# A mixer's small jobs in another order on five queues: where each stands among sixteen steps

## The reference, cut to what matters

```python
h = _layernorm(x, axis=-1) * (1 + ca) + sa
x = x + ga * _L1_attn_ref(h, ...)      # linear attention: elu(q)+1, elu(k)+1
h = _layernorm(x, axis=-1) * (1 + cb) + sb
x = x + gb * _L1_ffn_ref(h, ...)
# _L1_ffn_ref:
src = x + _gqa(x, ...)                 # softmax attention, 16 heads, 4 key heads
src = _rmsnorm(src, norm1_w)
src = src + _moe(src, ...)             # top 2 of 8 experts, capacity 2560, order of tokens counts
return _rmsnorm(src, norm2_w)
```

## Time and profile before

| what | value |
|---|---|
| time, median of 3 runs | 3388.16 us |
| lowest and highest | 3386.55, 3393.27 us |
| the profiled execution's own time | 3381.69 us |
| its span in the profile | 3380.0 us |
| mean granted clock of TensorE | 0.972 |
| busy: TensorE, DVE, ACT, POOL | 93%, 62%, 49%, 33% |

### The profile page before, as it was taken

How to read it: one execution, slowest core, us unless ns; L and a number is a source line. 1 busy time by engine, 2 the same in 40 slices (tenths; PEclk the granted TensorE clock), 3 DMA queues, 4 the chain that set the end, 5 groups by cost and what they waited for, 6 DMA issues and landing times. The chain is left out here.

```text
span 3380.0 us, 58015 instructions
## 1 busy us (share of the span) xinstructions
PE 3143.3 (93%) x18353; PEld 1931.6 (57%) x18353; DVE 2079.9 (62%) x5622; ACT 1663.7 (49%) x3743; POOL 1117.2 (33%) x1508
## 2 busy tenths in 40 slices
PE   6899999999998976999999999999999859999997
PEld 3566767677665653344444444444444348888882
DVE  6777777777771234777777777777777632222226
ACT  3555565555541113666666666666666611111116
POOL 2122232222343123334444444444442322222224
PEclk8999999999999988999999999999999969999998
DMA  8110010101125951112222222222222137677758
GB/s 281 12 73 36 36 72 36 72 36 36 72 81 188 308 184 29 54 54 72 74 73 73 74 73 73 73 68 73 73 72 70 52 101 239 226 239 235 223 169 299
DMA packets 266210, 370.48 MB, mean 110 GB/s; under 512 B 41615, under 2 KB 201579, under 8 KB 263904
## 3 DMA queue, kind: packets, MB, share of 16 engines
q1 hardware_dynamic: 250592, 329.82, 30.3%
q0 software_dynamic: 14832, 34.57, 2.8%
q10 hardware_dynamic: 544, 3.15, 0.2%
HBM read 242.38 MB, written 130.39 MB: 110 GB/s over the span
## 5 line engine op out<-in xcount | busy, mean ns | idle before, releaser
L2415 ACT ACTIVATE pT<-psum 128x512 f32<-128x512 f32 x1024 | 599.4, 599 | 354.4 <-PE psum L3166 343.5
L2699 DVE TENSOR_REDUCE negmax<-psum 128x2 f32<-128x1024 f32 x512 | 624.7, 1220 | 204.5 <-PE psum L3136 198.5
L3166 PE MATMUL psum<-q_stack,k_stack 99*128 99x512 bf16 x1024 | 380.4, 385 | 7.7 <-ACT pT L2415 5.7
L3136 PE MATMUL psum<-k_stack,q_stack 96*128 96x512 bf16 x1024 | 309.6, 384 | 54.5 <-DVE negmax L2699 34.7
L935 ACT ACTIVATE probs<-probs,negmax 128x256 f32<-128x256 f32 x512 | 252.8, 495 | 140.1 <-DVE negmax L1027 136.3
L3482 ACT ACTIVATE actT_x<-psum 128x512 f32<-128x512 f32 x142 | 84.8, 597 | 445.1 <-PE psum L3548 445.1
L3512 DVE COPY ye<-psum 128x512 f32<-128x512 f32 x71 | 49.1, 691 | 400.5 <-PE psum L3560 400.5
L3178 PE MATMUL psum<-pT,v_tile 128*32 128x512 f32 x2048 | 276.2, 612 | 0.7 <-ACT pT L2415 0.7
L3470 POOL DMA_INDIRECT chosen_out<-ye,place x142 | 139.9, 985 | 401.2 <-DVE ye L3512 240.8
L3548 PE MATMUL psum<-xT_x,w_x 128*128 128x256 f32 x1136 | 259.2, 382 | 0.0
L3560 PE MATMUL psum<-w_x,actT_x 128*128 128x256 f32 x1136 | 256.6, 379 | 0.0
(11 more groups left out here) (389 smaller groups left out, 5869.7 us busy)
## 6 DMA issues: line engine op xcount, KB each, us to landing
w_x<-in_L_ffn_w_dram SPq DMA_DIRECT2D x142, 512.0 KB, 4.5
w_e<-in_L_ffn_w_dram SPq DMA_DIRECT2D x46, 1024.0 KB, 7.3
q_stacks<-q_part SPq DMA_DIRECT2D x192, 128.0 KB
q_stack<-q_stacks SPq DMA_DIRECT2D x64, 384.0 KB, 3.6
padded<-w_e SPq DMA_DIRECT2D x32, 645.0 KB, 5.7
xe<-padded SPq DMA_DIRECT2D x71, 258.0 KB, 4.0
gate_rows<-mods SPq DMA_DIRECT2D x66, 256.0 KB, 3.4
chosen_out<-w_e SPq DMA_DIRECT2D x16, 1024.0 KB, 7.6
```

The costliest lines, as they stand in the source:

```text
L2415: act.activation(pT[:, 4 * (s % 2) + r, :], bank(m, 2 + n % 2), ACT.Exp, scale=float(DHQ) ** -0.5)\
L2699: dve.tensor_reduce(negmax[:, p // 2, h:h + 2], m.psum[:, at:at + 2, :], AX.X, ALU.max, negate=True)\
L3136: mm = pe.matmul(bank(m, at + j), q_stack[0:K_SCORE, h, t * P:(t + 1) * P], k_stack[0:K_SCORE, g, :], start=True, stop=True)
L3166: pe.matmul(bank(m, 2 + n % 2), k_stack[:, g, kc * P:(kc + 1) * P], q_stack[:, REP * g + r, :], start=True, stop=True).then_inc(sT_done, 1)
```

## The change

Nothing is computed otherwise. In the five lists of `mixer_block` the jobs stand in another order; a moved job is at another step, or at another of the places within a step. On POOL, the first query features of a batch and `last_part` of its first queries now stand at the end of the body before, and the last scatter stands behind them. On DVE, `place` stands in step 6 (it was step 4), and `add_load` at the end of the body before. On SP, `store_keys` and a `max_rows` stand at the end of the body before, and `store_src` gets a wait for the store of the batch before. The diff, cut to these and to some of the other moves:

```diff
--- before.py
+++ after.py
@@ -2067,38 +2067,41 @@
             def store_src(b, par):
                 sp.wait_ge(src_ready, b * NT + NT)
+
+                if isinstance(b, int) and b > 0:
+                    sp.wait_ge(src_out, b * 16)
                 sp.dma_start(src_dram[bass.ds(b * S, S), :].rearrange("(t p) d -> p t d", p=P), src[:, par, :, 0:D])\
                     .then_inc(src_out, 16)
             def body(b, par, part):
-                if part(0):
-                    max_rows(b, 2)
-                if part(1):
-                    store_keys(b + 1)
                 if part(1):
                     load_stack(b + 1, 0)
+                if part(1):
+                    load_stack(b + 1, 1)
                 if part(0):
                     max_rows(b, 3)
                 if part(1):
-                    load_stack(b + 1, 1)
+                    max_rows(b + 1, 0)
                 if part(1):
-                    max_rows(b + 1, 0)
+                    store_second(b + 1)
+                if part(1):
+                    load_stack(b + 1, 2)
                 if part(1):
                     load_h2_rows(b + 1)
                 if part(1):
-                    store_second(b + 1)
+                    load_stack(b + 1, 3)
                 if part(3):
                     load_rows(b + 3)
                 if part(1):
-                    load_stack(b + 1, 2)
+                    max_rows(b + 1, 1)
                 if part(-1):
                     store_src(b - 1, 1 - par)
-                if part(1):
-                    load_stack(b + 1, 3)
-                if part(1):
-                    max_rows(b + 1, 1)
                 if part(2):
                     store_first(b + 2)
+                if part(1):
+                    max_rows(b + 1, 2)
+                if part(2):
+                    store_keys(b + 2)
             sp.dma_start(got1.rearrange("p t k d -> p t (k d)"), chosen_out0[S * TOPK:2 * S * TOPK, :]
                          .rearrange("(t p k) d -> p t (k d)", p=P, k=TOPK)).then_inc(got1_in, 16)
@@ -2242,49 +2245,49 @@
             def body(b, par, part):
                 if part(1):
-                    last_part(b + 1, 0)
+                    last_part(b + 1, 1)
+                if part(2):
+                    add_bias(b + 2)
+                if part(2):
+                    key_features(b + 2, 1)
+                if part(2):
+                    key_features(b + 2, 0)
                 if part(-2):
                     scatter(b - 2, par, 0)
                 if part(2):
-                    add_bias(b + 2)
-                if part(1):
-                    last_part(b + 1, 1)
+                    query_features(b + 2, 0)
+                if part(2):
+                    key_features(b + 2, 2)
                 if part(-2):
                     scatter(b - 2, par, 1)
+                if part(2):
+                    key_features(b + 2, 3)
                 if part(-2):
                     scatter(b - 2, par, 2)
                 if part(-2):
                     scatter(b - 2, par, 3)
-                if part(2):
-                    query_features(b + 2, 1)
+                if part(3):
+                    normalise_first(b + 3)
+                if part(0):
+                    hidden_rows(b, par)
                 if part(-2):
                     scatter(b - 2, par, 4)
+                if part(1):
+                    last_part(b + 1, 2)
                 if part(2):
-                    query_features(b + 2, 0)
-                if part(2):
-                    key_features(b + 2, 0)
-                if part(2):
-                    key_features(b + 2, 1)
-                if part(2):
-                    key_features(b + 2, 2)
+                    add_branch(b + 2, 0)
                 if part(-2):
                     scatter(b - 2, par, 5)
                 if part(2):
-                    key_features(b + 2, 3)
+                    add_branch(b + 2, 1)
                 if part(-2):
                     scatter(b - 2, par, 6)
-                if part(0):
-                    hidden_rows(b, par)
-                if part(1):
-                    last_part(b + 1, 2)
+                if part(2):
+                    last_part(b + 2, 0)
                 if part(3):
-                    normalise_first(b + 3)
+                    query_features(b + 3, 1)
                 if part(-2):
                     scatter(b - 2, par, 7)
-                if part(2):
-                    add_branch(b + 2, 0)
-                if part(2):
-                    add_branch(b + 2, 1)
             for b in range(-3, 2):
                 body(b, b % 2, lambda k: 0 <= b + k < B)
@@ -2444,21 +2447,17 @@
                         exps(b, s, 0)
-                    if s == 5 and part(1):
-                        second_part(b + 1, 0)
...
                     if s == 9 and part(2):
-                        key_value_parts(b + 2, 3)
...
-                    if s == 15 and part(2):
+                        key_exp(b + 2, 3)
...
@@ -2467,50 +2466,25 @@
-                    if s == 6 and part(2):
-                        query_exp(b + 2, 1)
...
+                    if s == 7 and part(2):
+                        query_exp(b + 2, 0)
...
-                        exps(b, s, 2)
-                    if s == 5 and part(1):
-                        first_part(b + 1, 1)
...
-                    if s == 7 and part(2):
-                        query_exp(b + 2, 0)
...
@@ -2518,21 +2492,50 @@
-                        exps(b, s, 3)
+                        exps(b, s, 2)
+                    if s == 2 and part(2):
+                        query_exp(b + 2, 1)
...
+                    if s == 5 and part(1):
+                        first_part(b + 1, 1)
...
+                        exps(b, s, 3)
-                    if s == 9 and part(2):
-                        key_exp(b + 2, 3)
...
+                    if s == 8 and part(2):
+                        key_value_parts(b + 2, 3)
...
@@ -2856,93 +2859,93 @@
                     maxima(b, 2 * s, part)
                     if s == 0 and part(1):
-                        second_stats(b + 1, 1)
...
+                    if s == 0 and part(-2):
+                        read_rank(b - 2)
...
-                    if s == 8 and part(-1):
-                        residual(b - 1, 1)
...
-                    maxima(b, 2 * s + 1, part)
-                    if s == 0 and part(-2):
-                        add_load(b - 2)
...
-                    if s == 1 and part(-2):
-                        read_rank(b - 2)
...
-                    if s == 4 and part(-2):
-                        place(b - 2, par)
...
-                    if s == 5 and part(1):
-                        part_remainder(b + 1, 1)
...
+                    maxima(b, 2 * s + 1, part)
+                    if s == 0 and part(1):
+                        second_stats(b + 1, 1)
...
+                    if s == 5 and part(1):
+                        part_remainder(b + 1, 1)
...
+                    if s == 6 and part(-2):
+                        place(b - 2, par)
...
+                    if s == 7 and part(-1):
+                        residual(b - 1, 1)
...
-                    if s == 15 and part(2):
-                        second_stats(b + 2, 0)
...
+                    if s == 15 and part(-1):
+                        add_load(b - 1)
...
@@ -3250,12 +3253,22 @@
                         scoresT(b, s, 0)
                     maxima(b, 2 * s, part)
-                    if s == 0 and part(2):
-                        transpose_hidden(b + 2, 0)
...
+                    if s == 7 and part(-1):
+                        project2(b - 1, 0)
...
                         scoresT(b, s, 1)
@@ -3265,58 +3278,48 @@
                     if s == 0 and part(2):
+                        transpose_hidden(b + 2, 0)
...
+                    if s == 0 and part(2):
                         transpose_hidden(b + 2, 1)
...
+                        scoresT(b, s, 2)
+                    maxima(b, 2 * s + 1, part)
+                    if s == 1 and part(-1):
+                        transpose_weighed(b - 1, 1)
...
+                    if s == 6 and part(-1):
+                        transpose_o2(b - 1, 1)
...
+                    if s == 6 and part(2):
+                        keys_values(b + 2, 2)
...
+                    if s == 9 and part(2):
+                        key_values_sum(b + 2)
...
                     if s == 11 and part(2):
-                        key_values_sum(b + 2)
...
-                        scoresT(b, s, 2)
-                    maxima(b, 2 * s + 1, part)
-                    if s == 5 and part(-1):
-                        transpose_o2(b - 1, 1)
...
-                    if s == 7 and part(-1):
-                        project2(b - 1, 1)
...
-                    if s == 7 and part(2):
-                        keys_values(b + 2, 2)
...
                         scoresT(b, s, 3)
@@ -3327,24 +3330,24 @@
-                    if s == 2 and part(-1):
```

(92 more changed lines are left out.)

199 lines of the change are left out of this document (71 added, 128 removed).

## The result

The changed kernel takes 3564.11 us (median of 4 runs, 3557.12 to 3572.17). The kernel before took 3390.72 us on the same chip (4 runs). The ratio is 1.0511, 95% interval [1.0492, 1.0531]: 173 us slower. The prediction said 3510, 3440 to 3565. The sign and the place were right, and the size was 50 us short: the time lies inside the range by only 1 us. How much of that is luck is told behind the experiments.

What follows compares the result with a forecast made beforehand. TensorE, busy 93% of the span, was taken as the bound. Main wait with its clock 99, keys' stack 11, first stack 1 and small ones 14 sum to 125 us, giving 3507 profiled, 3513 as median, stated as 3510; range 3440 to 3565.

Steps and rivals of the forecast that it cites:

- The wait: DVE's place waits for POOL's last scatter, held behind query features awaiting ACT's step 7 exp; 11 bodies, chance 0.80.
- the stall: TensorE's second max scores of step 7 held up by the late place on DVE: 6.9 us lost a body.
- The clock: TensorE's clock falls to half in its pause of 6.7 us: 2.1 us lost a body, bounds 0 and 4.3.
- the rival in which the clock stays low much longer: TensorE's slow clock persists after the pause: up to 10 us more a body, 3600 us; chance 0.05.
- The keys' stack: Keys' last_part behind the query features makes TensorE's pair 20 wait 3.6 us in bodies 0 to 2: 11 us.
- the small ones: Small TensorE waits from other moved jobs, less idle regained: +1.0 us in some 14 bodies, 14 us in all.
- the 0.4 us for the sum's wait: TensorE's sum of keys and values, two steps earlier, waits 0.4 us a body.
- the side-by-side transposes: On TensorE, the second transpose_hidden, now next to the first, waits for modulate: +1.1 us a body.
- `transpose_weighed(·,1)`: A small wait on TensorE at this job, estimated at 0.4 us a body.
- The ramp: Stretch ahead of the first softmax: the first keys' stack about 1 us later in body -1.

Runs made afterwards that it cites:

- e1: Changed kernel with ACT's query_exp(b+2,0) moved from step 7 to step 3: ratio 1.0083 to the kernel before.
- e2: Changed kernel with POOL's scatter(b-2,7) moved ahead of last_part(b+2,0) and query_features(b+3,1): ratio 1.0145 to the kernel before.
- e3: Changed kernel with DVE's place moved from step 6 to step 8: ratio 1.0237 to the kernel before.
- e4: Changed kernel with POOL's add_bias(b+2) moved behind scatter(b-2,3): ratio 1.0407 to the kernel before.
- e12: Changed kernel with add_bias(b+2) behind scatter(b-2,3) only in bodies below 0: ratio 1.0490 to the kernel before.
- e6: Changed kernel with query_exp(b+2,0) in step 3 and transpose_hidden(b+2,0) back at the start of step 0: ratio 1.0069 to the kernel before.
- e5: Changed kernel with TensorE's key_values_sum moved from step 9 to the head of step 10: ratio 1.0452 to the kernel before.
- e7: Changed kernel with query_exp(b+2,0) in step 3, transpose_hidden(b+2,0) at the start of step 0, key_values_sum heading step 10: ratio 1.0017 to the kernel before.

## Why the prediction was right, and where it was short

*The wait: shown.* Each step of it stands in the trace, in exactly 11 bodies. Moving ACT's job (e1), POOL's scatter (e2) or place (e3) removed it each time.

*Its size: the stall, 6.9 us a body, was mis-sized.* TensorE's wait was to be 6.7 us and is 9.6 to 10.0, 106 us in all and not 74. In the body shown the landing took 1.9 us (2087.44 to 2089.36) where I had 1.5. Place was costed at the 1.25 of the earlier trace rows, where POOL had nothing beside it; here it took 3.9, because the wait lined it up with add_bias. With add_bias away (e4) the wait is 7.0 to 7.4. The Trainium skill ("SBUF — State Buffer", Who interferes with whom) states this: a VectorE instruction with two inputs in SBUF contends with a GpSimd instruction that reads SBUF, and the second to start blocks until the first ends. The trace agrees: `ranked` reads `chosen` and `rank`, while the readings of PSUM kept their 1.22 us in every kernel. Here it stood until the fourth of add_bias's instructions was over, not only the one in flight.

*The clock: the term of 2.1 us was nearly right, and a second one was missing.* In the body shown the fall came 5.1 us after TensorE stopped (2084.89 to about 2090) and full speed 5.3 us after it worked again. Over the 11 bodies the clock fell in each stop and cost 2.4 us a body by the estimate above, 26.5 where the prediction had 23. The 13 further stretches at half clock, 25.1 us, weren't foreseen in any term; the nearest is the rival in which the clock stays low much longer, at 0.05.

*The keys' stack: the sum was right by luck.* Bodies 0 to 2 grew by 10.3 us, where 11 and 1.0 each of the small ones were forecast. But the stack was to stop TensorE for 3.6 us in all three, and did so in two: 3.7 us in body 0, where 1.8 stood before the change, and 2.4 in body 1:

```profile
1515.38 0.60 PE L3139 MATMUL psum<-k_stack,q_stack 96*128 96x512 bf16 x2 [2.44 <-DMA k_stack<-k_stacks]
```

In body 2, which grew most, TensorE doesn't wait for the stack. It waits for the key features, priced at 0.4, and then the sum comes in pieces and the clock is at half for about 10 us:

```profile
1602.52 0.91 PE L3052 MATMUL psum<-v_one,k_exp 128*32 128x33 f32 x45 [2.59 <-POOL k_exp L2159]
```

In e2 and e3 the stack cost 0.3 us a body and nothing. The step that failed in this term is the 0.4 us for the sum's wait: where POOL's queue is late, the key features are 2.6 us late or more, and their wait covers that for the stack.

*The small ones: +1.0 a body was short.* Of its parts, the side-by-side transposes measured 1.0 (I had 1.1) and `transpose_weighed(·,1)` 0.16 (0.4). What I had at 0.4, the sum of keys and values, has 15.3 us of gaps in the 11 bodies, and busy time is 16 us longer than in e12, where the sum is whole and seven further stretches at half clock are left (13 here). Where it is whole, cut_max takes the place of the gaps, 1.4 us a body (e1, e12): that collision with POOL I hadn't counted either. So much of the unforeseen clock comes with the pieces, and by e1 to e6 and e12 these are no matter of the job's place alone; the program or the chip is behind them, and the runs don't say which.

*The ramp: a missed step.* I gave 1 us to what lies ahead of the first softmax and looked at add_bias only in the steady bodies, where POOL's idle covers it. Ahead of them POOL is on the chain. The profiled execution lost 10.6 there; the comparison of e12 with e2, e3 and e5 gives add_bias about 5 of it.

The sum over the 11 bodies: the long stop 106.2 us, the transposes 10.5, the gaps 15.3 and smaller waits 10.4 are the 142.4 of idle; less the 33.9 of before that is 108.5. The clock in the stops 26.5, in the further stretches 25.1 and 0.9 besides are the 52.5 of busy time. The prediction had 76 + 23 for the stop and its clock and 11 of its 14 for the rest. Beside them: bodies 0 to 2 10.3 (it had 14 with their small ones), the ramp 10.6 (1). So the main wait was right by its mechanism. That the time still fell inside the range, by 1 us, is luck: some 50 us of the loss (the gaps 15.3, the further stretches at half clock 25.1, and the ramp but for 1) were in no term of the sum.

## What to carry to other kernels

When jobs move on in-order queues, follow each counted wait to the last job that raises the count, on its own engine: one exp in step 7 held POOL, DVE and with them TensorE, and moving it alone gave back 5/6 of the loss. Price a job that a wait will shift by what runs beside it then: here a VectorE instruction with two SBUF inputs stood until four GpSimd instructions were over. Profile the same program on a second chip before a difference of 20 us is given to an edit. And read the ramp by itself: an engine with 48 us of idle in a steady body can be the bound there.

## What the runs showed of the hardware

- `ranked` (128x64, two SBUF inputs) takes 0.21 us alone (the kernel before) and 1.6 to 3.0 beside POOL's add_bias (the 11 bodies of the changed kernel, e1, e6 and e7); a cast of 128x16 (0.18 us alone) took 1.76 beside POOL's tensor instructions in e7.
- A run of 64 small matmuls on TensorE came out in four pieces with gaps of about 0.47 us in each of the 11 bodies of two programs and whole in five others with the order of the first. Every program measured on one chip had gaps, none on two others. In the body shown the clock fell to half for some 3 us behind them. Their cause wasn't found.
- Around a stop of TensorE of 9.6 to 10.0 us the granted clock was 0.50 for 10 to 14 us, 3.3 to 6.3 of them while it worked, in each of the 11 bodies of the changed kernel.
- In the body shown, the waiter of an indirect scatter was released 1.9 us after the end of the instruction.
- The mixer began at 1253.8 to 1263.7 us in these executions with the same work ahead of it: one pair of profiles can't tell 10 us of a kernel apart, and the medians are needed.
